# A macaron block: attention's qkv as three bfloat16 products of rows transposed by DMA

## The reference

```
x = x + 0.5 * ffn(layernorm(x))        # shared FFN (hidden 2048) + 2 of 8 routed experts
x = x + attn(layernorm(x))
x = x + 0.5 * ffn(layernorm(x))

attn: tok = x.reshape(B, H*W//16, 16)                  # 16 neighbours of a row are one token
      qkv = (tok @ qkv_w).reshape(B, -1, 3, 16)        # qkv_w: 16 x 48
      x1, x2 = window attention in strips 1 x 8 and 8 x 1, 8 channels each, plus a 3x3 depthwise conv of v
      att = concat(x1, x2) @ proj_w + proj_b
      tok = tok + layernorm(att) * ln_w + ln_b         # transposed back to B x 512 x 512
```

## Time and profile before

| | |
|---|---|
| median of three runs | 1472.89 us |
| lowest, highest | 1470.03, 1473.58 us |
| profiled execution, span from first to last instruction | 1469.7 us |
| TensorE busy, matmul records | 1419.1 us, 7642 |
| VectorE, ScalarE, GpSimd busy | 944.8, 552.4, 501.0 us |

### The profile page before, as it was taken

The page is one execution under the profiler, slowest core; times in us unless marked ns, Lnnn a source line. Parts: engine busy times, 40 slices in busy tenths (PEclk is TensorE's granted clock), DMA queues, the critical chain, the costliest instruction groups (busy, mean ns, idle before and its releaser), DMA issues.

```text
span 1469.7 us, 22015 instructions
## 1 busy us (share of the span) xinstructions
PE 1419.1 (97%) x7642; PEld 679.7 (46%) x7642; DVE 944.8 (64%) x1295; ACT 552.4 (38%) x1153; POOL 501.0 (34%) x424
## 2 busy tenths in 40 slices
PE   4999999999999999899999999999999999999998
PEld 2444444444444544445454444444444444444443
DVE  5778853333348989898889889979925733333243
ACT  4566323333233433345435454345233213333211
POOL 2321132221244475252625434444322122221353
PEclk9999999999999999999999999999999999999999
DMA  8999659887493467075526552445338168888594
GB/s 305 305 350 320 267 146 209 200 182 192 172 277 125 156 196 220 30 244 135 153 72 186 150 166 73 121 160 140 112 101 257 59 188 213 192 190 185 187 321 165
DMA packets 233724, 272.63 MB, mean 186 GB/s; under 512 B 132242, under 2 KB 156818, under 8 KB 230162
## 3 DMA queue, kind: packets, MB, share of 16 engines
q1 hardware_dynamic: 198594, 166.34, 39.7%
q10 hardware_dynamic: 23664, 67.66, 14.5%
q0 software_dynamic: 11360, 37.23, 9.4%
HBM read 168.39 MB, written 72.88 MB: 164 GB/s over the span
## 4 chain that ended last, share of the span: by engine, by line
PE 63%; DVE 10%; issue 8%; DMA 4%; POOL 2%; ACT 2%; SPq 1%; POOLq 0%; ACTq 0%; DVEq 0%
PE bank L1484 25%; PE bank L1607 13%; PE bank L1498 12%; PE bank L1632 7%; DVE region L1147 3%; DMA rows<-sorted_y,slots 1%; PE side L1120 1%; PE side L1620 1%; DVE region L1153 1%; POOL rows L665 1%; DMA x2d<-rows 1%; DVE sgh L1854 1%; PE side L1253 1%; DMA region<-region 1%; POOL hs L1812 1%
## 5 line engine op out<-in xcount | busy, mean ns | idle before, releaser
L1484 PE MATMUL bank<-xT,wb 128*128 128x512 bf16 x2688 | 615.5, 381 | 22.6 <-DMA xT<-region 17.6
L1484 PEld LDWEIGHTS bank<-xT,wb 128*128 128x128 bf16 x2688 | 257.7, 98 | 323.9 <-issue 29.2
L1812 POOL TENSOR_TENSOR hs<-sgh,hs 128x512 bf16<-128x512 f32 x126 | 161.9, 1285 | 629.1 <-ACT hs L1704 628.2
L1498 PE MATMUL bank<-wb,hs 128*128 128x512 bf16 x1536 | 358.0, 380 | 0.2 <-POOL hs L1812 0.2
L1498 PEld LDWEIGHTS bank<-wb,hs 128*128 128x128 bf16 x1536 | 147.8, 98 | 173.9 <-issue 2.9
L1607 PE MATMUL bank<-wr,region 128*128 x912 | 221.7, 379 | 0.0
L1704 ACT ACTIVATE hs<-sgh 128x512 bf16<-128x512 f32 x128 | 81.3, 635 | 340.2 <-DVE sgh L1854 337.4
L1854 DVE TENSOR_TENSOR sgh<-bank,sgh 128x512 f32<-128x512 f32 x128 | 87.9, 687 | 155.8 <-PE bank L1484 154.6
L1147 DVE TENSOR_TENSOR region<-region 128x1024 f32<-128x1024 f32 x128 | 183.0, 1454 | 0.9
L1801 POOL DMA_INDIRECT region<-xnd,idxs x78 | 74.6, 957 | 221.8 <-DMA region<-region 213.5
L1153 DVE TENSOR_REDUCE region<-region 128x256 f32<-128x2048 f32 x64 | 146.3, 2286 | 2.2
(11 more groups left out here) (182 smaller groups left out, 1351.6 us busy)
## 6 DMA issues: line engine op xcount, KB each, us to landing
wb<-wsplit ACTq DMA_DIRECT2D x42, 1024.0 KB
wb<-wsplit ACTq DMA_DIRECT2D x42, 512.0 KB, 4.4
sorted_y<-region SPq DMA_DIRECT2D x78, 256.0 KB
wsplit<-wb SPq DMA_DIRECT2D x8, 1536.0 KB, 7.4
wr<-wall SPq DMA_DIRECT2D x6, 1536.0 KB, 9.7
rows<-x SPq DMA_DIRECT2D x32, 256.0 KB, 4.9
region<-xln SPq DMA_DIRECT2D x128, 64.0 KB, 3.7
xnd<-rows SPq DMA_DIRECT2D x30, 256.0 KB, 4.0
```

Source lines behind the costliest of these rows:

```text
L1484: m = e.matmul(ps[:], wb[:, w % 2, wp, at:at + P], xt[:, xp, c, :], start=(i == 0), stop=(i == 3 * NDC - 1))
L1498: m = e.matmul(psD[tt][:], hs[:, s % 2, hp, tt * P:(tt + 1) * P], wb[:, w % 2, wp, at:at + D], start=(first and i == 0), stop=(last and i ...
L1812: e.tensor_tensor(hs[:, s % 2, 1, :], sgh[:, s % 2, :], hs[:, s % 2, 0, :], ALU.subtract).then_inc(S("h_lo").sem, 1)
```

## The change

The normalized rows are also written in parts: a new tensor `xlp` holds for each 128 columns of a row 128 bfloat16 high parts and 128 low parts, in the bytes of 128 floats. `sp_load` loads these instead of `xln2` (eight DMAs of the same size). One slot later (d-3) `sp_turn` transposes `sco` to `tok` with two DMA transposes of 128 x 1024 bfloat16, and the qkv pieces make three bfloat16 products of 64 rows and 192 columns for each one of float32. `wqkv` is kept as two bfloat16 parts, made with the other constants. The turn pieces, their ScalarE copies and their PSUM use are gone. For the parts, `Combine` gains a second scaling and a subtraction on VectorE for its first four tiles, `Evac` 2 to 4 a copy on ScalarE and a subtraction on VectorE for each of four tiles, and each a store. The first half's qkv pieces stand later (slot 27 place 5, slot 28 places 1, 3, 5). The tiles of images 0 and 1 of `Prep` start two slots and one slot later, the loads of `Evac` 4 and 5 move by +2 and +1 slot, and the planner's shares count the new work, which moves some of `WORKS` by a slot.

```diff
-        wqkv = sb("wqkv", [P, 4 * 3 * C])
+        wqkv = sb("wqkv", [P, 2, 4 * 3 * C], BF16)
...
-                if self.low_rows:
+                if self.low_rows or self.i < 2:
                     evacuated(e, 3 + self.i)
...
+        def halves_of(t):
+            return t.bitcast(BF16).rearrange("p (c h n) -> p c h n", c=NDC, h=2)
...
+            def act_high(self, e, k):
+                for tt in (2 * k, 2 * k + 1):
+                    e.wait_ge(S("ev_ln").sem, 4 * self.k + tt + 1)
+                    e.activation(halves_of(T(4 + tt))[:, :, 0, :], chunks_of(T(tt)), ACT.Copy).then_inc(S("ev_hi").sem, 1)
+
+            def vec_low(self, e, k):
+                for tt in (2 * k, 2 * k + 1):
+                    e.wait_ge(S("ev_hi").sem, 4 * self.k + tt + 1)
+                    both = halves_of(T(4 + tt))
+                    e.tensor_tensor(both[:, :, 1, :], chunks_of(T(tt)), both[:, :, 0, :],
+                                    ALU.subtract).then_inc(S("ev_lo").sem, 1)
...
                 if self.ln:
-                    e.wait_ge(S("c_ln").sem, self.m + 1)
+                    e.wait_ge(S("c_lo").sem, self.m + 1)
+                    e.dma_start(xlp[self.rows, :], self.b).then_inc(S(f"c_out{self.q}").sem, 16)
...
                 e.wait_ge(S("c_rstd").sem, self.m + 1)
+                e.tensor_scalar(both[:, :, 0, :], chunks_of(self.r), mv[:, q, 0:1], rstd[:, q, :], ALU.subtract,
+                                ALU.mult).then_inc(S("c_hi").sem, 1)
...
+            def vec_low(self, e):
+                both = halves_of(self.b)
+                e.wait_ge(S("c_hi").sem, self.m + 1)
+                e.wait_ge(S("c_ln").sem, self.m + 1)
+                e.tensor_tensor(both[:, :, 1, :], chunks_of(self.a), both[:, :, 0, :],
+                                ALU.subtract).then_inc(S("c_lo").sem, 1)
...
-            PIECES += [(d - 2, m, "turn", h, m) for m in range(2)]
-            PIECES += [((d - 2, 3), (d - 2, 5), (d - 1, 2), (d - 1, 5))[k] + ("qkv", h, k) for k in range(PAIRS)]
+            at = ((d - 2, 3), (d - 2, 5), (d - 1, 2), (d - 1, 5)) if h else ((d - 2, 5), (d - 1, 1), (d - 1, 3), (d - 1, 5))
+            PIECES += [at[k] + ("qkv", h, k) for k in range(PAIRS)]
...
+            def sp_turn(self, e):
+                h = self.h
+                e.wait_ge(S("t_x").sem, HALF_MOVES * (h + 1))
+                if h >= 2:
+                    e.wait_ge(S("t_out").sem, h - 1)
+                elif h == 1:
+                    e.wait_ge(S("side_made").sem, piece("qkv", 0, PAIRS - 1))
+                else:
+                    e.wait_ge(S("x3_kept").sem, 16)
+                for m in range(2):
+                    cols = slice(m * 512, (m + 1) * 512)
+                    e.dma_start(self.tok[:, cols].bitcast(BF16).rearrange("p (c n) -> p c n", c=WL),
+                                self.sco[:, cols].bitcast(BF16), transpose=True).then_inc(S(f"t_turned{m}").sem, 16)
...
             def pe_qkv(self, e, k, ps):
-                e.wait_ge(S("side_read").sem, piece("turn", self.h, k // 2))
+                if self.h == 0 and k == 0:
+                    e.wait_ge(S("bias_moved").sem, 96)
+                e.wait_ge(S(f"t_turned{k // 2}").sem, 16 * (self.h + 1))
                 for n in range(2):
                     g = 2 * k + n
-                    for b in range(2):
-                        rows = slice(64 * b, 64 * b + 64)
-                        mm = e.matmul(ps[:, b, n * 192:(n + 1) * 192], self.tok[rows, g * P:(g + 1) * P], wqkv[rows, :],
-                                      start=True, stop=True, skip_group_check=True)
+                    for i, (wp, xp) in enumerate(PASSES):
+                        for b in range(2):
+                            rows = slice(64 * b, 64 * b + 64)
+                            mm = e.matmul(ps[:, b, n * 192:(n + 1) * 192], self.tokb[rows, g, xp, :], wqkv[rows, wp, :],
+                                          start=(i == 0), stop=(i == 2), skip_group_check=True)
                 mm.then_inc(S("side_made").sem, 1)
...
                 def slot(s):
+                    for h in range(HALVES):
+                        if s == D_SLOT[h] - 3:
+                            Half(h).sp_turn(e)
...
                     for ev, k in evac_ln_at(s - 2):
                         ev.act_norm(e, k)
+                        ev.act_high(e, k)
...
+                    for ev, k in evac_ln_at(s - 3):
+                        ev.vec_low(e, k)
```

More of the change, by code:

```diff
@@ L92, in macaron @@
     xln2 = nc.dram_tensor("xln2", [ROWS, D], F32).ap()
+    xlp = nc.dram_tensor("xlp", [ROWS, D], F32).ap()
     attd = nc.dram_tensor("attd", [ROWS, D], F32).ap()
@@ L560, in sp_load @@
                         n = NT + 4 * (v - 4) + 2 + tt % 2
+                        if v == 4 and tt < 2:
+                            kept(e, n - 2)
+                            crossed(e, n - 2)
+                            e.wait_ge(S("side_made").sem, piece("third", n - 2))
                         if tt < 2:
@@ L908, in attention_constants @@
             o.do(e.tensor_tensor(pbf[0:1, :], pbf[0:1, :], bprod[0:1, :], ALU.add))
+            o.do(e.tensor_copy(wqkv[:, 0, :], wqf))
             o.sync()
+            o.do(e.tensor_tensor(wqkv[:, 1, :], wqf, wqkv[:, 0, :], ALU.subtract))
             yield
@@ L1008, in macaron @@
         SHARE = {"scores": (1.3, 3.5), "values": (1.4, 3.6), "max": (1.5,), "sums": (0.7, 1.3), "merge": (2.8,)}
-        PE_SHARE = {"third": 0.3, "logits": 0.5, "turn": 0.7, "qkv": 0.7, "back": 0.7, "proj": 1.2, "out": 0.7}
+        PE_SHARE = {"third": 0.3, "logits": 0.5, "qkv": 0.7, "back": 0.7, "proj": 1.2, "out": 0.7}
         def share(w):
@@ L1066, in __init__ @@
                 s0 = 8 * q
-                self.img = xln2[image, :].rearrange("r c -> (r c)").rearrange(
-                    "(s i g e) -> s g i e", s=16, i=WL, g=16)[s0:s0 + 8]
+                self.img, self.parts = (a[image, :].rearrange("r c -> (r c)").rearrange(
+                    "(s i g e) -> s g i e", s=16, i=WL, g=16)[s0:s0 + 8] for a in (xln2, xlp))
+                self.tokb = self.tok.bitcast(BF16).rearrange("p (g w n) -> p g w n", g=WL, w=2)
                 self.res = attd[image, :].rearrange("r c -> (r c)").rearrange(
@@ L1363, in const_load @@
                         j = t % 4
-                        w6 = wqkv[part, :].rearrange("p (a n) -> p a n", a=6)
+                        w6 = wqf[part, :].rearrange("p (a n) -> p a n", a=6)
                         q6 = qkvw.rearrange("p (a c) -> p a c", a=6)
@@ L1527, in sides @@
                             bias_product(e, ps)
-                        elif kind == "turn":
-                            Half(n).pe_turn(e, m, ps)
                         elif kind == "qkv":
@@ L1676, in sides @@
                             e.activation(bprod[0:1, :], ps[0:1, 0:64], ACT.Copy).then_inc(S("side_read").sem, 1)
-                        elif kind == "turn":
-                            Half(n).act_turn(e, m, ps)
                         elif kind == "qkv":
```

47 lines of the change are left out of this document (22 added, 25 removed).

## The result

The changed kernel takes 1478.14 us (median of 20 runs, 1473.53 to 1484.94), the kernel before in the same rounds 1474.5: ratio 1.0028, 95% interval 1.0018 to 1.0038. Predicted were 1461.6 us and a range of 1455 to 1471. By the prediction's own bound of 0.3% the difference is hardly told from no change, to which it gave a chance of 0.15, but the interval leaves no room for a gain. The profiled execution took 1482.28 us with a span of 1480.5, so it is one of the slower ones; single figures read from it are of that execution.

The account below looks back on a forecast made before the run. TensorE, busy 97% of the span, was taken as the bound. Terms -7.0 - 5.9 - 5.4 + 2.4 + 1.3 + 0.7 + 1.6 + 1.0 = -11.3 us took the span from 1469.7 to 1458.4, the median to 1461.6; range 1455 to 1471.

Parts of the forecast that it names:

- what is late next: First half: 2.4 us more wait for VectorE's multiplication, then 1.3 us for the transposed rows, clock 0.
- TensorE's pieces: All eight halves: removed turn pieces save 7.0 us; 32 qkv pieces at 0.77 instead of 0.955 save 5.9.
- Rival A: Qkv pieces: weight loads of the 64-row products not hidden, 1.35 us a piece, 1480.3 us in all; chance 0.08.
- Waits that go: TensorE's waits for rows a transpose reads (3.3 us) and ScalarE's copy of transposed rows (2.2) vanish: 5.4 us.
- First combines, 2.4: Two combines ahead of slot 25's multiplication each gain a scaling and a subtraction on VectorE: 2.4 us more wait.
- Half 0's rows, 1.3: First qkv piece of half 0: TensorE waits 1.3 us for DMA transposes landing 3.2 or 4.8 us after issue.
- Half 5, 0.7: First qkv piece of half 5, the tightest later half: TensorE waits 0.7 us for transposed rows, bounds 0 and 3.
- Clock, 0: First half: the slow-clock cost of 1.5 us moves to the new 3.4 us wait, net 0, bounds -1.5 and +1.5.
- Half 2's merge, 1.6: What half 2 saves ahead of its late VectorE merge comes back as TensorE wait: 1.6 us.
- Copies behind the evacuations, 1 us; stores and moved tiles, nothing: 12 ScalarE copies and 12 VectorE subtractions mostly hide, 1 us, bounds 0 and 5; xlp stores and later slots cost nothing.
- Rival B: Halves 0 and 5: transposes need 8 us, TensorE waits some 3 us more each, clock falls: 1470.6 us; chance 0.10.
- Rival C: VectorE becomes the bound; halves 3 to 7 lose their 1.6 us as half 2 does: 1469.7 us; chance 0.09.

Follow-up runs that it names:

- direct: The changed kernel without its 16 DMA transposes, the qkv products reading the loaded rows themselves: 1478.0 us.
- late5: The changed kernel with a separate semaphore for the parts' store, combine 3's load before half 0's loads, combine 4's right behind, half 5's qkv pieces later: 1471.6 us.
- noparts: The changed kernel without the arithmetic that makes the stored parts; stores, loads and DMA transposes stay: 1471.7 us.
- both_out: The changed kernel without the DMA transposes and without the arithmetic of the parts; third store and moved slots stay: 1469.2 us.
- after_late5: The changed kernel with one edit, half 5's four qkv pieces at later places in slots 70 and 71: 1477.1 us.
- stall_lo: The kernel before with five added waits of TensorE, ahead of down products, for GpSimd's low part: 1496.1 us, ratio 1.0130.

## Why the prediction was wrong, by its steps

In the prediction's own terms the sum was -11.3 us: pieces -12.9, waits that go -5.4, waits that come +7.0, clock 0. Read from the profile of after it is -15.0, -5.4 and +20, and over all runs +5.7 for the clock. That makes +5, where the runs say +3.6. So the step that failed is the one on what is late next, with the clock behind it.

- *TensorE's pieces*: the turn pieces' 7.0 right; the qkv pieces saved 8.0, not 5.9. With 0.49 us of columns a piece has 0.22 of overhead, not 0.28, and the plain scaling by passes (0.72) was nearer than the sum (0.77). Rival A's row halves, each with its weight loads in the open, did not come. (The 12 products from 967.33 fill 2.68 us up to the piece, by the row, not 2.59; the 0.216 us each is right all the same, the 24 from 984.10 give it.)
- *Waits that go*, 5.4: right.
- *First combines, 2.4*: right in mechanism and nearly in size. Slot 26 waits 2.96 us, by 1.97 more than before, for VectorE's multiplication. That a stall of this length has a stretch at 1.2 GHz behind it was not priced.
- *Half 0's rows, 1.3*: **failed**. The wait was 4.66. The step let the DMA transposes land in 3.2 to 4.8 us as in the earlier trace rows; the two of half 0 took 7.2 and 6.0, at a DMA share of 1.00. (The share alone doesn't tell: from 571 to 576 us it was 1.11, and half 2's two landed in 3.7 and 3.6.) And it said that the combines' loads behind them "wait for VectorE anyway"; they were issued 4.3 us later in their slot, and VectorE's multiplication behind them came later too. direct shows that this second chain is as long as the first.
- *Half 5, 0.7*: **failed** in the same way, 4.2 (landed 7.8 and 7.1 us after issue). Here too a second chain, VectorE's merge, is about as long (direct, late5).
- *Clock, 0*: **failed**, the largest single term: +5.7 us over all runs. The text moved the one stretch of the earlier trace rows instead of asking at how many places TensorE would now wait as long as the 3.10 us that stand ahead of it in the earlier trace rows. In the changed kernel's profile there are five of about that length (2.96, 4.66, 2.67, 4.22, and 3.73 at 1396.15 for VectorE's multiplication), and each has its stretch. Against before, half 0 has two stretches' worth more (10.2 us for 3.4) and half 5 one: 5.1 us, nearly all of the 5.7.
- *Half 2's merge, 1.6*: right in size, by luck. Half 2 gained nothing net (slots 43 to 46), but the wait at the merge did not grow to 4.5 us, it is 2.67; TensorE waits 1.04 and 0.89 us for VectorE's multiplication in slots 43 and 44 instead.
- *Copies behind the evacuations, 1 us; stores and moved tiles, nothing*: **failed**. noparts says 6.4 us for all arithmetic of the parts. In its profile slot 26 gains 1.97, but slots 26 to 28 together only 0.4; half 5 gains 4.8, as its transposes land sooner. So most of what the runs put on the arithmetic isn't VectorE's time in a slot, and its way to TensorE stays open. The stores, put at nothing, cost 2 to 7 us. Moved tiles put two waits for ScalarE (0.92 and 1.16) into slots 61 and 62, though putting them back won nothing.

Rival B described what the trace shows (waits of 4.7 and 4.2 with 1.2 GHz behind them) and had 1470.6 for it; as the only cause it fell with direct, where both waits are gone and the time is the same. Rival C is half right: VectorE is the next limit in half 5 and takes back half 2's gain, but the halves 3, 6 and 7 kept 1.9, 0.9 and 1.9 us of TensorE's gain in their own slots.

Left open: why the store costs 7 us in one arrangement and 2 in the other; what makes a transpose land late; where in half 0 the 4.6 us of both_out come from, beyond the 2.6 that go with the store; and why slots 1, 3 and 118, alike in all these kernels, have a slow stretch in some executions. In the changed kernel's profile these three have 13.7 us at 1.2 GHz, which cost up to 6.8.

## What to carry to other kernels

When TensorE is 97% busy, price each new wait twice: by its length, and, where it is as long as one that has a slow stretch behind it in the trace, by half of that stretch; a placement that shortens such a wait can be worth that (1.7 us here) even where the net stays. When a store, a load and a transpose are added to a queue in order, follow everything queued behind them to the engine that it feeds, since the next chain was only a little shorter. Work moved to an engine in order costs by its place in that order: 16 subtractions of 0.67 us, 10.8 us of work, made 17.0 us of waits.

## What the runs showed of the hardware

With waits of TensorE of 3.1 us and more a stretch at 1.2 GHz came in 33 of 34 cases in the profiles of this case (not at 3.14 us in after_late5), 3.4 us long or a multiple; with those of 2.6 to 3.1 in 14 of 20; with 2.0 to 2.6 in 24 of 74, and not each time at the same place; with 1.5 to 2.0 in 2 of 43; with 1.0 to 1.5 in none of 107. The Trainium skill (TensorE: Matmul & The Clock Gate, "HAM oscillation — how this bites in real kernels") tells that waits for data between bursts bring the clock down; stall_lo agrees, and shows it for a wait on another engine, once with the DMA engines idle throughout.

One of the two DMA transposes of a half (128 x 1024 bfloat16) landed 3.4 to 3.8 us after issue in halves 2 and 3, 3.5 and 5.2 in half 7, and 6.0 to 12.6 in halves 0, 1 and 5; its issue held SyncE's queue for 1.2 to 1.3 us in halves 2, 3 and 7 and for up to 4.5 in halves 0, 1 and 5. The profile's own summary for half 0 and half 2:
```profile
DMA to landing us min/median/max: 6.0/6.6/7.2
DMA to landing us min/median/max: 3.6/3.7/3.7
```
A float32 piece of four products of 64 rows costs 0.955 us, its three bfloat16 passes 0.705.
